# Row 0 of a two-layer graph network in parts of 128, 128 and 256 nodes, row 1 in halves, with the blocks of columns 0 and 1 taken two rows at a time

## What is computed

```
h = relu(layernorm(x))
x = x + adj @ (h * (u >= 0.1) / 0.9)          # layer 1
h = relu(layernorm(x))
x = x + adj @ (h @ W) + b                     # layer 2
```

## Time and profile before

| | |
|---|---|
| runs | 886.42, 886.44, 886.90 us, median 886.44 |
| profiled execution | 886.64 us, its span 884.8 us |
| TensorE busy | 865.8 us, 98% of the span |
| VectorE / ScalarE busy | 564.6 us (64%) / 42.6 us (5%) |
| transfers | 361.62 MB, mean 409 GB/s |
| chain that ended last | TensorE 83%, DMA 10%, VectorE 4%, SyncE's queue 2% |
| TensorE's granted clock | 1.000 of full speed |

### The profile page before, as it was taken

The page is one execution under the profiler, slowest core; times in us unless marked ns, Lnnn a source line. Parts: engine busy times, 40 slices in busy tenths (PEclk is TensorE's granted clock), DMA queues, the critical chain, the costliest instruction groups (busy, mean ns, idle before and its releaser), DMA issues.

```text
span 884.8 us, 13364 instructions
## 1 busy us (share of the span) xinstructions
PE 865.8 (98%) x5484; PEld 490.0 (55%) x5484; DVE 564.6 (64%) x1193; ACT 42.6 (5%) x120; POOL 1.4 (0%) x11
## 2 busy tenths in 40 slices
PE   6799999999999999999999999999999999999998
PEld 5445444444445464465547576666757655567543
DVE  5364633323244548586868686978778898798724
ACT  3100000000000000000000000000000000000000
POOL 0000000000000000000000000000000000000000
PEclk9999999999999999999999999999999999999999
DMA  9999999999999999999999999999999999999993
GB/s 374 420 420 419 422 421 421 420 420 421 422 390 420 421 420 421 418 421 421 419 421 419 420 420 416 416 420 405 420 412 414 392 410 420 419 422 419 418 419 114
DMA packets 52316, 361.62 MB, mean 409 GB/s; under 512 B 5792, under 2 KB 6048, under 8 KB 10016
## 3 DMA queue, kind: packets, MB, share of 16 engines
q1 hardware_dynamic: 52096, 360.73, 98.8%
q10 hardware_dynamic: 160, 0.03, 0.0%
HBM read 358.65 MB, written 2.10 MB: 408 GB/s over the span
## 4 chain that ended last, share of the span: by engine, by line
PE 83%; DMA 10%; DVE 4%; SPq 2%; issue 1%; ACT 0%; DVEq 0%
PE banks L790 30%; PE banks L816 22%; PE row_sums L765 17%; DMA blocks<-in_adj 10%; PE banks L784 6%; PE row_sums L822 5%; PE banks L800 3%; SPq L469 2%; DVE acc L659 0%; PE banks L917 0%; DVE quarters L635 0%; PE banks L884 0%; DVE quarters L631 0%; DVE blocks L633 0%; DVE x L584 0%
## 5 line engine op out<-in xcount | busy, mean ns | idle before, releaser
L790 PE MATMUL banks<-blocks,features 128*64 128x512 f32 x1248 | 379.7, 593 | 0.3 <-DMA blocks<-in_adj 0.3
L765 PE MATMUL row_sums<-blocks,features 128*64 128x512 f32 x984 | 241.8, 592 | 0.6 <-DMA blocks<-in_adj 0.5
L790 PEld LDWEIGHTS banks<-blocks,features 128*64 128x64 f32 x1248 | 128.3, 137 | 134.3 <-issue 131.9
L673 DVE TENSOR_TENSOR acc<-acc,banks 128x512 f32<-128x512 f32 (+1 forms) x106 | 72.6, 685 | 140.1 <-PE banks L790 128.7
L816 PE MATMUL banks<-quarters,mixed 128*64 128x256 f32 x664 | 157.6, 379 | 0.4
L765 PEld LDWEIGHTS row_sums<-blocks,features 128*64 128x64 f32 x984 | 93.0, 137 | 104.6 <-issue 99.0
L784 PE MATMUL banks<-blocks,features 128*64 128x512 f32 x272 | 119.7, 592 | 0.2 <-DMA blocks<-in_adj 0.2
L816 PEld LDWEIGHTS banks<-quarters,mixed 128*64 128x64 f32 x664 | 90.6, 137 | 27.5 <-DVE quarters L641 2.1
L816 PE MATMUL banks<-quarters,features 128*64 128x256 f32 x332 | 85.4, 380 | 0.0
L816 PE MATMUL banks<-blocks,features 128*64 128x256 f32 x332 | 85.3, 379 | 0.1
L822 PE MATMUL row_sums<-blocks,mixed 128*64 128x256 f32 x332 | 85.3, 379 | 0.0
(11 more groups left out here) (63 smaller groups left out, 594.8 us busy)
## 6 DMA issues: line engine op xcount, KB each, us to landing
blocks<-in_adj SPq DMA_DIRECT2D x337, 1024.0 KB, 13.7
x<-in_x SPq DMA_DIRECT2D x2, 1024.0 KB, 7.3
acc<-in_u SPq DMA_DIRECT2D x2, 1024.0 KB, 9.4
out<-x SPq DMA_DIRECT2D x7, 256.0 KB, 2.3
blocks<-in_adj SPq DMA_DIRECT2D x2, 512.0 KB, 26.5
out<-x SPq DMA_DIRECT2D x2, 128.0 KB, 1.8
w_twice<-in_wb ACTq DMA_DIRECT2D x2, 16.2 KB, 6.0
```

The source lines that it names most:

```text
L673: nc.vector.tensor_tensor(mine, mine, banks[at, q.bank, :], ALU.add).then_inc(sum_added, 1)
L765: return nc.tensor.matmul(row_sums[at, t.unit % 2, nodes], features[:, tile_of(k, j), 0:D], tile, start=start, stop=last and t.n == unit_l ...
L790: return nc.tensor.matmul(banks[at, t.sum.bank, nodes], features[:, tile_of(t.k, j), D:2 * D], tile, start=t.n == t.sum.first and j == t.t ...
```

## The change

- Row 0 becomes three units of 128, 128 and 256 nodes (words `h`, `i`, `j`), row 1 two of 256 (`k`, `l`). A load of a part of 128 nodes holds four columns' parts, one of 256 two columns'. Every later row stays one unit.
- Columns 0 and 1 are taken ahead in the same parts: words `t`, `u` (column 0, tiles 0 and 1), `v` (its tiles 2 and 3), `w`, `x` (column 1, tiles 0 and 1, tiles 2 and 3). Such a word now works on two rows, and the sums of layer 1 and of layer 2 of both rows go to a bank each; each is added with one instruction of 128 partitions.
- The first loads of columns and rows leave out what the other border has already brought (`skipped`).
- The head of `ORDER` is rewritten up to row 2's words; from there on the words are the same, but `p0.4` is gone and `r0.4` comes in after `r0.6`.
- Blocks of row 0 that are loaded again come by two transfers (pieces of 2 KiB and 4 KiB a partition; before 4 KiB), those of row 1 in pieces of 4 KiB (before 8 KiB). Layer 2 of row 0 is three products a tile (before two), of row 1 two (before one).

```diff
-HALVES = 2
-UNITS = BLOCKS + 1
+SPLIT = [[range(0, 1), range(1, 2), range(2, TILES)], [range(0, 2), range(2, TILES)]]
+UNIT = [(i, tiles) for i in range(BLOCKS) for tiles in (SPLIT[i] if i < len(SPLIT) else WHOLE)]
+UNITS = len(UNIT)
+GROUP = [[TILES // len(tiles) for tiles in parts] for parts in SPLIT]
...
-h0 h2 h4 h6 h8 h10 h12 h14 i6 i8 i10 i12 t1 t2 t3 t4 t5 t6 t7 t8 t9 t10 t11 t12 t13 t14 t15 i14 i4 i2 i0 o1.6
-o1.7 o1.8 o1.9 o1.10 m0.5 u1 u2 u3 u4 u5 u6 u7 u8 u9 u10 u11 u12 u13 u14 u15 o1.11 o1.12 o1.13 o1.14 o1.15
-o1.4 o1.3 o1.2 o1.1 o2.6 o2.7 o2.8 o2.9 p0.1 b2.1 a3.1 a4.1 a5.1 a6.1 a7.1 o2.10 a8.1 o2.11 a9.1 o2.12 a10.1
-o2.13 o2.14 a11.1 o2.15 a12.1 o2.5 a13.1 o2.4 a14.1 o2.3 a15.1 o2.2 o3.7 o3.8 o3.9 o3.10 o3.11 o3.12 m2.6 b3.2
+h4 h8 h12 h0 i4 i8 t0 t1 t2 t3 t4 t5 i12 i0 t6 t7 j14 j12 u0 u1 u2 u3 j10 j8 j6 u4 j4 j2 u5 j0 u6 u7 k4 v0 v1 v2
+v3 k6 k8 v4 k10 k12 k14 k2 k0 v5 v6 v7 m0.4 w1 l6 w2 l8 w3 l10 w4 l12 l14 w5 l2 l0 w6 w7 o2.6 p0.1 x1 o2.7 o2.8
+x2 o2.9 o2.10 x3 o2.11 o2.12 x4 o2.13 o2.14 x5 o2.15 o2.5 x6 o2.4 o2.3 x7 o2.2 o3.7 o3.8 o3.9 o3.10 o3.11 o3.12
...
-s4.3 p2.3 p0.3 o4.14 s4.2 o4.15 o4.7 o4.6 o4.5 o4.4 o5.9 o5.10 o5.11 o5.12 o5.13 o5.14 m4.8 s5.4 p2.4 p0.4
+o4.13 s4.3 p2.3 p0.3 o4.14 s4.2 o4.15 o4.7 o4.6 o4.5 o4.4 o5.9 o5.10 o5.11 o5.12 o5.13 o5.14 m4.8 s5.4 p2.4 s5.2
...
+r2.6 s8.7 p6.7 p4.7 s8.2 s8.3 s8.4 o8.11 s8.5 o8.10 s8.6 o8.9 o8.8 o9.13 o9.14 r0.6 r0.4 o9.15 o9.11 m8.12 s9.8
...
+            both_rows = len(t.operands) == 2
+            t.sum = Sum(t.row // 2, None if both_rows else t.row % 2, n)
+            if both_rows:
+                t.sum_x = Sum(t.row // 2, None, n)
+                t.sum_x.of_x, t.sum_x.last = True, n
+                sums.append(t.sum_x)
...
                 elif i == 0:
-                    to = blocks[:, slot, :].rearrange("p (h c) -> p h c", h=HALVES)
-                    of = adj[0:BLOCKS].rearrange("(h a) p (b c) -> a b p h c", h=HALVES, b=2)[k // 2, k % 2]
+                    at, n = 2 * P * TILES, GROUP[0][0]
+                    to = blocks[:, slot, 0:at].rearrange("p (h c) -> p h c", h=2)
+                    of = left_0[0:AT[0][2]].rearrange("(h a) p (b c) -> a b p h c", h=2, b=n)[k // n, k % n]
+                    sp.dma_start(to, of).then_inc(block_arrived[slot], 16)
+                    n = GROUP[0][2]
+                    to, of = blocks[:, slot, at:], left_0[AT[0][2] + k // n, :, k % n * at:(k % n + 1) * at]
...
-                mine = acc[at, q.p, :]
+                mine = (x1 if q.of_x else acc)[at, q.p, :]
...
+            def layer_1_of_part(t, load, q, half, last):
+                wide, (column, j) = width(t.unit), divmod(q, TILES)
+                start, started[t.unit, half] = not started[t.unit, half], True
+                return nc.tensor.matmul(row_sums[half * D:(half + 1) * D, t.unit % 2, 0:wide],
+                                        features[:, tile_of(load.k * GROUP[load.i][load.part] + column, j), 0:D],
+                                        blocks[:, load.slot, q * wide:(q + 1) * wide],
...
             def layer_2(t, operand, j, half):
-                (nodes, tile), = pieces(operand, t.k, j)
-                return nc.tensor.matmul(banks[at, t.sum.bank, nodes], features[:, tile_of(t.k, j), D:2 * D], tile,
+                for part, (nodes, tile) in enumerate(pieces(operand, t.k, j)):
+                    done = nc.tensor.matmul(banks[at, t.sum.bank, nodes], features[:, tile_of(t.k, j), D:2 * D], tile,
...
                 if s == 0:
-                    pe.wait_ge(xd_ready, t.k // 2 + 1)
+                    pe.wait_ge(xd_ready, (t.k + GROUP[0][m] - 1) // 2 + 1)
...
                         elif t.kind == "ahead":
-                            layer_1_ahead(t, j, 1 - s % 2)
-                            done = layer_2(t, t.operands[0], j, s % 2)
+                            for operand in t.operands:
+                                layer_1_ahead(t, operand, j, 1 - operand[0] % 2)
+                            for operand in reversed(t.operands):
+                                done = layer_2(t, operand, j, operand[0] % 2)
```

More of the change, by code:

```diff
@@ L96, in __init__ @@
         self.kind, self.operands, self.k, self.row, self.unit, self.tiles = kind, operands, k, row, unit, tiles
-        self.steps = 2 if kind == "one" else 3.5 if kind == "seven" else len(tiles)
-        self.needs = k + 2 if tiles.stop == TILES or k else 1
-        self.sum = None
+        self.steps = 2 if kind == "one" else 3.5 if kind == "seven" else TILES
+        if kind == "ahead":
+            self.steps = len(tiles) * len(operands)
+        if kind == "one" and operands[0][1][0].kind == "left":
+            self.steps = 2 * operands[0][1][0].size
+        self.needs = next(m + 1 for m in range(UNITS) if UNIT[m][0] == k and UNIT[m][1].stop >= tiles.stop)
+        self.sum = self.sum_x = None
     def loads(self):
@@ L155, in ordered @@
             i, k = numbers
-            items.append(Item({"o": "one", "b": "both", "s": "seven"}[kind], [operand(i, k)], k, i, i + 1))
+            items.append(Item({"o": "one", "b": "both", "s": "seven"}[kind], [operand(i, k)], k, i, FIRST_UNIT[i]))
     return items
@@ L176, in plan @@
         assert free[load.slot] < min(later.first for later in loads[n:]), "a block needs a slot that is still held"
-        count[load.slot] += 1
+        count[load.slot] += load.transfers
         load.before, load.arrived = holder[load.slot], 16 * count[load.slot]
@@ L306, in bass_gnn @@
      finals, rests_at) = plan()
-    closing = {q.last: q for q in sums}
+    closing = {q.last: [r for r in sums if r.last == q.last] for q in sums}
     final_of = {p: n for n, p in enumerate(finals)}
@@ L788, in layer_2 @@
                 at = slice(half * D, (half + 1) * D)
[L789 to L802 removed]
+                for part, (nodes, tile) in enumerate(pieces(operand, t.k, j)):
+                    done = nc.tensor.matmul(banks[at, t.sum.bank, nodes], features[:, tile_of(t.k, j), D:2 * D], tile,
+                                            start=t.n == t.sum.first and j == t.tiles[0] and part == 0,
+                                            stop=t.n == t.sum.last and j == t.tiles[-1], skip_group_check=True)
+                return done
             def seven(t):
@@ L858, in multiply @@
                         pe.wait_ge(sum_added, t.sum.before.done)
+                if t.sum_x is not None and t.sum_x.before is not None:
+                    pe.wait_ge(sum_added, t.sum_x.before.done)
                 arrived(t)
-                if s == 0:
-                    done = layer_1_of_half_row(t)
+                if t.kind == "one" and s < len(SPLIT):
+                    load, = t.loads()
+                    for q in products_of(load):
+                        done = layer_1_of_part(t, load, q, q % 2, q >= GROUP[s][load.part] * TILES - 2)
                 elif t.kind == "seven":
```

216 lines of the change are left out of this document (116 added, 100 removed).

## The result

The changed kernel takes 890.18 us (median of 5 runs, 889.91 to 890.25) against 886.44 before (5 runs, 886.31 to 886.9). The ratio is 1.004, with a 95% interval of 1.0025 to 1.0055: slower by 3.7 us, more than the 0.2% that can be told from no change. The profiled execution took 890.25 us, its span is 888.4.

A forecast was written before the change was run, and what follows sets the result against it. TensorE and the one block queue were both full, with block landings deciding at m4.8 and r4.8. +3.4 us at r4.8 and +0.5 for later row 0 words made +3.9 on 886.64, giving 890.5 us, range 886 to 896.

The forecast's parts named there:

- The start: Before m4.8: 128-node blocks take 1.79 us, t0 starts at 35.5 instead of t1 at 46.2, worth only 0.6 us.
- The estimate of 0.162 us: 128-wide instructions of row 0 by the skill's rule, instead of 0.112 us; the sum would be 896 instead of 890.5.
- The early gain is worth nothing: At m4.8: TensorE comes some 2 us sooner but waits there for the same 116th MiB.
- The waits between m4.8 and r4.8: At o6.15: about 1.6 of the 3.46 us gained by dropping p0.4 turns into a wait for its block.
- r4.8: Its block, two MiB later, lands at 507.7; the word starts at 508.0 instead of 504.6: +3.4 us.
- The term of pieces: Row 0's reloads in shorter pieces: 0.1 us for each of four items ahead of r4.8, bounds 0 to 0.75.
- The transfer decides at r4.8: At r4.8: TensorE alone would come at 506.2, the block lands at 507.7; total 890.5 us, chance 0.69.
- The later words of row 0: After r4.8: eight words carry row 0 in three parts, 0.07 us more each, +0.5 us.
- holes in the DMA row: Sign that the forecast is wrong: gaps in the transfers would mean too few slots are free; no size given.
- (a): Rival, faster: TensorE's idle time of the first 46 us is won back and kept; below 884.7 us, chance 0.10.
- (b): Rival, no change: queue pauses fall otherwise; one fewer ahead of r4.8 gives 888.9, two fewer 887.3 us; chance 0.13.
- (c): Rival, slower by TensorE: 128-wide instructions on half an array cost over 0.112 us, taken as 0.16; 896.6 us, chance 0.08.

The follow-up runs named there:

- e9_stand_in: Changed kernel without reload r0.4, with p2.4 done a second time at p0.4's old place (338 MiB, output not the reference's): 886.76 us, ratio 1.0.
- e2_r04: Kernel before the change with only p0.4 taken out and r0.4 put after r0.6, row 0 still in halves: 888.63 us, ratio 1.0021.
- e8_long: Changed kernel with reloaded blocks of rows 0 and 1 coming whole in 8 KiB pieces from another place (output not the reference's): 889.1 us, ratio 1.0028.
- e10_no_reload: Changed kernel with p6.8 a second time in place of r0.4, so two MiB are not loaded (output not the reference's): 888.84 us, ratio 1.0026.
- e5_fill: e4_alternate with four words needing no new block put ahead of four that wait for theirs, transfer order unchanged: 890.96 us, ratio 1.0046.
- e4_alternate: Changed kernel with the five products per tile of a row 0 pair issued in turn between its two rows: 889.62 us, ratio 1.003.
- e1_p04: Changed kernel with p0.4 back after p2.4 and r0.4 taken out (338 MiB): 917.64 us, ratio 1.0346.
- e3_r24: Changed kernel with p2.4 also taken out and r2.4 put after r0.4 (342 MiB): 895.95 us, ratio 1.0098.
- e7_fill_late: e5_fill with r4.8 and r4.10, and so their four blocks, also moved later in the order: 893.28 us, ratio 1.007.

## Why the prediction came out right

The forecast was 890.5 us and the time is 890.18. Point by point:

**Bytes.** The queue moved 362.83 MB instead of 360.73: the two MiB as counted.

**The start.** Full blocks of 128 nodes were forecast at 1.79 us; the chain of waits has two of them at the full clock, i12 and i0, as

```profile
44.18 3.49 PE row_sums L818 x64
```

that is 1.75 us each, or 0.109 us from one 128-wide instruction of a half to the next, where 0.112 was assumed. The first block, h4, took 2.67 us at a fallen clock (last section), which the prediction did not have; it was hidden, because h12 has to wait for VectorE's last pair of rows until 26.9 us. t0 started at 34.5, inside the 34 to 37 given and 1.0 before the 35.5 worked out, for the chain of unit 0 took 3.7 us (30.73 to 34.47) instead of the 4.6 allowed. The estimate of 0.162 us, worked out from the Trainium skill, "TensorE: Matmul & The Clock Gate", section "Back-to-back issue gap", does not hold for these pairs of instructions side by side, and the sum of 896 by it would have been wrong; the row on full-width products was the better guide.

**The early gain is worth nothing.** Right, and e9_stand_in shows it by itself: with the late work and bytes taken out, the new start and the parts come to 886.76 beside 886.64. The wait at m4.8 was forecast at about 2 us and is 1.37, because its block landed at 304.6 instead of 305.6. The queue lost less in pauses ahead of it: the slice at 390 GB/s of the kernel before, the twelfth, is at 421 in the changed kernel. In e2_r04, whose start is that of the kernel before, it is at 423, so it was not the change that took this pause away. In e9_stand_in m4.8 starts 0.8 us sooner than before, and the dearer words of row 0 behind it take that back.

**The waits between m4.8 and r4.8.** The step put 1.6 us at o6.15 (its own figures, 340.9 - 338.9 = 2.0 of the 3.46, give 1.5). It is 0.63 there, and 0.75 at m6.10 and 1.34 at r2.6, which the step did not name. Their sum, 2.7, is larger by 1.1, and m4.8's wait smaller by 0.6; TensorE came to r4.8 at 506.55, with 506.2 forecast.

**r4.8.** The block was forecast at 507.7 and landed at 507.24; the start at 508.0, and it was 507.37. So +2.75 instead of +3.4. The term of pieces was mis-sized: 0.1 us a word was taken, e8_long measures 0.3 for a pair of blocks, 0.9 us more for the four. That the landing came out early all the same is the 1.0 us that the queue was ahead at m4.8 already. Two errors of about 1 us cancelled here, and that was luck.

**"The transfer decides at r4.8."** Right as to the path, but it says less than it seems to. The forecast's own figures split +3.4 into 1.6 us by which TensorE alone would be late and 1.8 for the transfer. The runs split 3.4 us, of the end and not of r4.8's start, into 2.1 (e10_no_reload, work put off past words that wait) and 1.3 (the bytes). A reader who takes "the transfer decides" as "without the two MiB the loss is gone" is refuted by e10_no_reload; one who takes it as "TensorE's idle time ahead of r4.8 does not matter" is confirmed by e5_fill, where r4.8 started at the same moment with four waits filled.

**The later words of row 0.** +0.5 was forecast and +0.85 came. The products are not dearer than the step said; the sequence is: with the same products issued in turn the work behind r4.8's start takes about 0.5 us less (e4_alternate).

**What the prediction did not see** is why the change has to load column 4 again at all. It named holes in the DMA row as a sign of too few slots but did not ask what p0.4 would do to them; e1_p04 shows that the parts would have cost 31 us with it.

Of the rivals, (a), the idle time won back, is excluded by e9_stand_in and e5_fill; (b), pauses that fall otherwise, did happen (1.0 us at m4.8), and would have taken the time towards 889.5 if the pieces had cost what was assumed; (c), dear narrow products, is excluded by the row above. Left open: why a pause of the queue falls where it does. That was not tried. Of the kernel before and of the changed one there is one trace each, so the pauses of their other executions are not known.

## What to carry to other kernels

Where one queue is full from start to end, a head start of the compute engine ends at the next word whose block is late; count the blocks ahead of that word before counting what the head start saves. Work put off behind such waits is in part paid twice, once as idle time at the waits ahead and once where it is done (2.1 us for 3.5 us of work in e10_no_reload), so a reload belongs where blocks land well ahead of their words (here 1.5 us between two places of the same word). And a tile that spans more columns holds its slot until the last of them is used.

## What the hardware showed that was not expected

**The clock after a wait.** In e5_fill, r4.8 took 5.35 us instead of 3.65 after TensorE had idled 2.24 us. The granted clock around it, windows of e5_fill:

```profile
507.30:509.90 2.60, 2.60 (x8) 0.97 (x10) 2.50 (x5) 0.00 (x0) 0.00 (x0) 0.62 1.01 419
509.90:512.60 2.70, 2.70 (x12) 1.09 (x10) 0.01 (x1) 0.00 (x0) 0.00 (x0) 0.73 1.04 425
512.70:516.00 3.30, 3.30 (x32) 2.48 (x30) 3.27 (x8) 0.00 (x0) 0.00 (x0) 1.00 1.03 429
```

From 508 to 511 us it is 0.50 throughout, from 512 us on 1.00. So part of the word ran at 1.2 GHz and the rest at 2.4. The same happened after 2.05 us of idle in e3_r24 and after 2.11 us at r0.5 in e5_fill; it did not after 1.91 us at m4.8 in e4_alternate, nor after 1.98 us at r0.5 in e7_fill_late, nor after 3.04 us at o6.15 in e3_r24, where this row is followed by products at full speed:

```profile
337.05 1.94 PE L810 MATMUL row_sums<-blocks,features 128*64 128x512 f32 x8 [3.04 <-DMA blocks<-in_adj]
```

The length of the idle time alone does not say when the clock falls; what else does, these runs leave open. At r4.8 a fall costs 1.7 us, nearly as much as the wait itself, so one long wait can be dearer than the four short ones that it replaces. The changed kernel has a fall too, at its start, where TensorE waits for VectorE; h4's block, and the window around it:

```profile
18.95 2.67 PE L818 MATMUL row_sums<-blocks,features 128*64 128x128 f32 x32 [3.87 <-DVE features L598]
```

```profile
18.00:36.00 18.00, 15.04 (x200) 13.14 (x202) 11.91 (x31) 3.47 (x12) 0.00 (x0) 0.81 1.01 419
```

The clock is 0.50 from 22 to 24.8 us and 1.00 again from 27 us on. The kernel before, whose waits for blocks up to 46 us were 0.5 to 1.4 us each, stayed at 1.00 between 18 and 36 us.

**Halves in sequence.** Two products on different halves of the array run side by side, but with three products of one half ahead in the sequence the other half runs late, 0.22 us more behind r0.6 and r0.4 than with the products issued in turn (e4_alternate). Over the words behind r4.8 this came to about 0.5 us.

**Slots and rate.** With five of the 18 slots held up to 350 us where three were held before, and five more up to p0.3, the queue fell from 420 to 189 GB/s in one slice of e1_p04; the kernel has no room for even a few slots that stand idle.
